# Second attention: two tiles of maxima and one unit in three PSUM banks, VectorE reduces maxima bank by bank

## The reference

```python
qkv = xn @ w_qkv
...
q = q * scale
sim = jnp.einsum('bhid,bhjd->bhij', q, k)
attn = jax.nn.softmax(sim, axis=-1)
out = jnp.einsum('bhij,bhjd->bhid', attn, v)
out = jnp.transpose(out, (0, 2, 1, 3)).reshape(b, n, DIM_INNER)
return out @ w_out
```

## Time and profile before

| what | us |
|---|---|
| median of 3 runs (lowest to highest) | 1211.06 (1207.18 to 1211.94) |
| the profiled execution, its own time | 1208.63 |
| its span from the first to the last instruction | 1206.8 |
| TensorE (PE) busy | 1151.7 (95%) |
| VectorE (DVE) busy | 843.3 (70%) |
| GpSimd (POOL) busy | 775.8 (64%) |
| ScalarE (ACT) busy | 597.7 (50%) |

### The profile page before, as it was taken

One profiled execution on the slowest core, in us unless ns is written; L12 is line 12 of the kernel. 1 busy time (PEld: TensorE's weight loads), 2 busy tenths in 40 slices (PEclk: granted clock), 3 DMA queues, 4 the chain that ended last, 5 costly groups with the idle time before them and its releaser, 6 DMA issues.

```text
span 1206.8 us, 21785 instructions
## 1 busy us (share of the span) xinstructions
PE 1151.7 (95%) x8892; PEld 731.1 (61%) x8892; DVE 843.3 (70%) x1086; ACT 597.7 (50%) x930; POOL 775.8 (64%) x495
## 2 busy tenths in 40 slices
PE   7999999998887899999999999999999999899997
PEld 6899999876664445454444544544445445457776
DVE  4765886565566577787777777778778787865553
ACT  1543334546553645555554555546555455554342
POOL 3565776753433678878878788898888888840000
PEclk9998999998998999999999999999999999999999
DMA  6000000020000020000000000000000000000000
GB/s 206 2 2 2 3 2 2 2 72 1 1 1 1 1 95 2 1 1 1 1 1 1 1 1 1 2 1 1 1 1 1 1 1 1 1 1 10 9 9 9
DMA packets 6978, 13.65 MB, mean 11 GB/s; under 512 B 1744, under 2 KB 4176, under 8 KB 6496
## 3 DMA queue, kind: packets, MB, share of 16 engines
q1 hardware_dynamic: 6096, 11.66, 2.9%
q10 hardware_dynamic: 784, 0.61, 0.2%
HBM read 11.22 MB, written 1.05 MB: 10 GB/s over the span
## 4 chain that ended last, share of the span: by engine, by line
PE 85%; DVE 8%; ACT 3%; issue 3%; ACTq 1%; POOL 0%; DVEq 0%; POOLq 0%
PE o_ps L1335 19%; PE mx_ps L1294 8%; PE ha_banks L494 7%; PE st_ps L1314 5%; PE st_ps L1317 5%; PE st_ps L1320 5%; PE bank L1693 3%; PE pj_ps L1246 3%; PE pj_ps L1265 3%; PE bank L1695 3%; PE bank L1694 3%; PE pj_ps L1257 2%; PE ha_banks L558 2%; PE ha_banks L511 2%; PE pj_ps L1240 2%
## 5 line engine op out<-in xcount | busy, mean ns | idle before, releaser
L1609 POOL TENSOR_TENSOR acc<-acc,prob 128x1024 f32<-128x1024 f32 x192 | 466.3, 2429 | 77.4 <-ACT prob L1456 68.5
L1518 DVE TENSOR_REDUCE mx_part<-mx_ps 128x2 f32<-128x1024 f32 x251 | 300.4, 1197 | 145.6 <-PE mx_ps L1294 145.6
L1456 ACT ACTIVATE prob<-st_ps 128x1024 f32<-128x1024 f32 x256 | 248.6, 1023 | 226.3 <-PE st_ps L1320 226.3
L1335 PE MATMUL o_ps<-prob,v_cur 128*64 128x512 f32 x1024 | 244.8, 599 | 0.0
L1294 PEld LDWEIGHTS mx_ps<-k_hi,q_hi 64*128 64x128 f32 x502 | 47.2, 184 | 142.3 <-issue 98.1
L1294 PE MATMUL mx_ps<-k_hi,q_hi 64*128 64x512 f32 x502 | 122.8, 485 | 8.8 <-DVE mx_part L1518 8.4
L1335 PEld LDWEIGHTS o_ps<-prob,v_cur 128*64 128x64 f32 x1024 | 65.5, 136 | 97.6 <-issue 90.8
L1534 DVE RECIPROCAL rden<-rden 128x128 f32<-128x128 f32 x128 | 120.3, 942 | 2.6 <-ACT rden L1420 2.6
L1609 POOL TENSOR_TENSOR acc<-prob 128x1024 f32<-128x1024 f32 x32 | 76.0, 2375 | 51.9 <-PE pj_ps L1242 31.2
L1320 PE MATMUL st_ps<-q_hi,d_lo 64*128 64x512 f32 x512 | 101.3, 391 | 0.0
L752 POOL TENSOR_TENSOR ha_wide<-ha_pt,ha_own 128x512 f32<-128x512 f32 x64 | 73.8, 1185 | 8.6 <-ACT ha_pt L709 8.6
(11 more groups left out here) (364 smaller groups left out, 2207.3 us busy)
## 6 DMA issues: line engine op xcount, KB each, us to landing
h_w<-in_h SPq DMA_DIRECT2D x2, 1024.0 KB, 8.0
w_raw<-in_w SPq DMA_DIRECT2D x8, 192.0 KB, 3.6
x<-in_x SPq DMA_DIRECT2D x4, 256.0 KB, 6.4
head_wkv<-in_wkv SPq DMA_DIRECT2D x1, 1024.0 KB, 10.6
out<-fin SPq DMA_DIRECT2D x4, 256.0 KB, 2.3
m_w<-in_m SPq DMA_DIRECT2D x3, 256.0 KB, 2.8
sel_raw<-in_sel SPq DMA_DIRECT2D x1, 576.0 KB, 11.3
ha_head_pos<-in_pos ACTq DMA_DIRECT2D x2, 256.0 KB, 7.8
```

Source lines behind the costliest of these rows:

```text
L1335: mm = pe.matmul(o_ps[rows(h), :], v_cur[:, m % 2, j, rows(h)], prob[:, (16 * m + slot) % RING, h, :], start=(j == 0), stop=(j == KT - 1), ...
L1456: act.activation(prob[:, n % RING, :, :], st_ps[:, slot % 2, :, :], ACT.Exp, scale=SCALE).then_inc(s_exp, 1)
L1518: dve.reduce_max(mx_part[:, :, i, keys:keys + 1], maxima_banks(q, n), AX_X).then_inc(s_mxr, 1)
L1609: pool.tensor_tensor(total, old, new, ALU.add).then_inc(s_acc, 1)
```

## The change

A batch with m of at least 1 and b not 0 or 4 is "three" (the rule `three`), up to the last tile of maxima: 6 batches in each of the steps 1 to 14 and 2 in step 15, 86 in all. In these:

- the first tile of maxima goes into `mx_ps` banks 0 and 1 as before;
- the second goes into `mx_ps` bank 0 and `pj_ps`. It waits for the reduction of bank 0 of the first tile alone (`first_out`) and for the former reader of `pj_ps`;
- the early unit goes into bank 1 of `mx_ps` (`aside`), and waits for the whole reduction of the first tile;
- the first tile of the batch after waits for both, the reductions and the reader of the early unit;
- VectorE reduces each of the four banks by an instruction of its own, 128x512.

All other batches are as they were. Since `pj_ps` has another order of users, `pj_uses` takes the place of `turns` in `bank_free`.

```diff
+    def three(m, b):
+        return m >= 1 and b % (BATCHES // 2) != 0 and BATCHES * m + b < BATCHES * (STEPS - 1) + 3
...
+    def batch_of(q, n):
+        return divmod(8 * q + n // 2 + 3 - BATCHES, BATCHES)
...
+    def apart(q, n):
+        return three(*batch_of(q, n))
...
+    first_out, all_out, count = {}, {}, 0
+    for q in range(STEPS):
+        for n in range(16):
+            first_out[q, n] = count + 1
+            count += 2 if apart(q, n) else 1
+            all_out[q, n] = count
...
     def tensor_unit(pe, q, u):
         p = q % PAIRS
-        to = pj_ps[:, :]
+        to = unit_bank(q, u)
...
+        elif aside(q, u):
+            pe.wait_ge(s_mxr, all_out[maximum(q - AHEAD[u], BEFORE.index(u), 0)])
         else:
             bank_free(pe, turn_of[q, u])
...
     def maxima_banks(q, n):
...
+        if n % 2 and apart(q, n):
+            return [mx_ps[:, 0, :], pj_ps[:, :]]
+        return [mx_ps[:, h, :] for h in range(2)]
...
     def tensor_maxima(pe, q, n):
...
+        elif n % 2 and apart(q, n):
+            pe.wait_ge(s_mxr, first_out[q, n - 1])
+            bank_free(pe, turn_of[q, ("max", n)])
         else:
-            pe.wait_ge(s_mxr, 16 * q + n)
+            pe.wait_ge(s_mxr, all_out[q, n] - (2 if apart(q, n) else 1))
+            was = divmod(8 * q + n // 2 + 2 - BATCHES, BATCHES)
+            if n % 2 == 0 and three(*was) and before(*was):
+                unit_out(pe, *before(*was))
...
     def vector_maxima(dve, q, n):
         i, keys = MX[n]
         dve.wait_ge(s_mx, 16 * q + n + 1)
-        dve.reduce_max(mx_part[:, :, i, keys:keys + 1], maxima_banks(q, n), AX_X).then_inc(s_mxr, 1)
+        if apart(q, n):
+            for h in range(2):
+                dve.reduce_max(mx_part[:, h, i, keys:keys + 1], maxima_banks(q, n)[h], AX_X).then_inc(s_mxr, 1)
+        else:
+            both = st_ps[:, 2 - n % 3, :, :] if q == 0 and n < 8 and n % 3 else mx_ps[:, :, :]
+            dve.reduce_max(mx_part[:, :, i, keys:keys + 1], both, AX_X).then_inc(s_mxr, 1)
```

More of the change, by code:

```diff
@@ L1154, in after, with maximum, maxima_there, unit_there @@
         return (q, AFTER[b]) if 0 <= q < STEPS else None
+    def maximum(m, b, second):
+        n = 2 * (BATCHES * (m + 1) + b - 3) + second
+        return (n // 16, n % 16) if 0 <= n < 16 * STEPS else None
+    def maxima_there(m, b):
+        if not three(m, b):
+            return None
+        q, n = maximum(m, b, 1)
+        return q, ("max", n)
+    def unit_there(m, b):
+        return None if three(m, b) else before(m, b)
     def norm_at(m, b):
         return [(LAST, ("norm", n)) for n in NORMS_AT.get((m, b), ()) if n in ("mean", "var", "spread", "rvar", "rspread")]
+    def three(m, b):
[10 more added lines that the diff above has]
+            all_out[q, n] = count
+    MXR_END = count
+    def aside(q, u):
+        if u not in BEFORE:
+            return False
+        b = BEFORE.index(u)
+        return three(q - AHEAD[u], b)
     turns = [(0, QK[3]), (0, QK[2]), (0, ("v", 0)), (0, ("v", 1)), (0, ("tr", 0))]
@@ L1163, in second_attention @@
               for u in [before(m, b), after(m, b)] + norm_at(m, b) if u]
[L1164 removed]
+    pj_uses = turns[:5]
+    pj_uses += [u for m in range(STEPS + 1) for b in range(BATCHES)
+                for u in [maxima_there(m, b), unit_there(m, b), after(m, b)] + norm_at(m, b) if u]
+    turn_of = {turn: n for n, turn in enumerate(pj_uses)}
     count_of = {turn: n + 1 for n, turn in enumerate([t for t in turns if t[1][0] != "norm"])}
[L1168 to L1171 removed]
     def half_of(half):
@@ L1245, in tensor_unit @@
                 for h in range(2):
-                    mm = pe.matmul(pj_ps[rows(h), tile(i)], xr[:, chunk(q, u[1]), i * P + h * HD:i * P + h * HD + HD],
+                    mm = pe.matmul(to[rows(h), tile(i)], xr[:, chunk(q, u[1]), i * P + h * HD:i * P + h * HD + HD],
                                    w_raw[:, p, W_QK:W_V], start=True, stop=True, skip_group_check=True)
@@ L1250, in tensor_unit @@
             for h in range(2):
-                mm = pe.matmul(pj_ps[rows(h), 0:P], mx_row[:, h, :], c.ident[:, :], start=True, stop=True,
+                mm = pe.matmul(to[rows(h), 0:P], mx_row[:, h, :], c.ident[:, :], start=True, stop=True,
                                skip_group_check=True)
@@ L1269, in maxima_banks @@
     def maxima_banks(q, n):
-        return st_ps[:, 2 - n % 3, :, :] if q == 0 and n < 8 and n % 3 else mx_ps[:, :, :]
+        if q == 0 and n < 8 and n % 3:
+            return [st_ps[:, 2 - n % 3, h, :] for h in range(2)]
+        if n % 2 and apart(q, n):
+            return [mx_ps[:, 0, :], pj_ps[:, :]]
+        return [mx_ps[:, h, :] for h in range(2)]
     def tensor_maxima(pe, q, n):
@@ L1385, in scalar_split, with unit_bank @@
         act.activation(w_hi[:, p, :], w_raw[:, p, 0:W_QK], ACT.Copy).then_inc(s_whi, 1)
-    def qk_bank(q, u):
-        return st_ps[:, 0, QK.index(u), :] if q == 0 and u in QK[:2] else pj_ps[:, :]
+    def unit_bank(q, u):
+        if q == 0 and u in QK[:2]:
+            return st_ps[:, 0, QK.index(u), :]
+        return mx_ps[:, 1, :] if aside(q, u) else pj_ps[:, :]
     def scalar_unit(act, q, u):
```

29 lines of the change are left out of this document (15 added, 14 removed).

## The result

The changed kernel takes **1190.23 us** (median of 4 runs, 1190.03 to 1191.22), the kernel before in the same comparison 1209.95 (1207.18 to 1211.94): a ratio of 0.984, 95% interval 0.9813 to 0.9868. The forecast was 1187, with a range of 1182 to 1198. Its profiled execution has a span of 1188.6 us against 1206.8.

A forecast was written before the change was run, and what follows sets the result against it. TensorE was taken to set the time, with losses between starts. Gains of 17.6 + 4.5 + 0.5 = 22.6 us gave 1186.0 from the profiled 1208.63, or 1188.5 from the median; 1187 was taken, range 1182 to 1198.

The forecast's parts named there:

- What bounds the kernel: Second attention: TensorE, busy for all 550 us, sets the time; the loss must come from times between starts.
- The second tile: Second tile of maxima in full batches: waiting for one bank's reduction wins 0.21 each, 84 times, 17.6 us.
- The early unit's cover of 0.16: Early unit in bank 1 of `mx_ps`: ready at 611.41, wanted at 611.57, so covered by 0.16, cost 0.
- `out`, 0.16 in 28 batches: Batches 3 and 7: `out` no longer waits for `q_max`, gaining 4.5 us, at most 1.4 us at risk.
- The next first tile: First tile of the batch after: waiting for the early unit's reader just fits, cost 0, bound 1.4 us.
- sign of being wrong: Early unit, `out` or batch 3's first tile beginning with idle time that a reduction or `q_lo` ended.
- VectorE's extra work: 172 instructions, each pair 0.06 to 0.12 longer, 10 to 20 us busy; no cost except through the releases.
- GpSimd: GpSimd's share rises from 84% to 87% as the step shrinks to about 41.4: cost 0, bound 1 us.
- Step 15: Two second tiles released 0.5 to 0.6 earlier each, but `den` then waits: 0.5 counted, bounds 0 and 1.1.
- A (1194): Rival on VectorE's split reductions: a half costs more than 0.60, such as 0.68; time 1194; chance 14%.
- B (1204): Rival on the second tile: it does not start earlier, only `out` gains 4.5 us; time 1204; chance 6%.

The follow-up runs named there:

- only_tile: The changed kernel with the rule `three` in batches 1, 2, 5 and 6 alone: 1201.32 us, ratio 0.9918 to the kernel before.
- short_first: The kernel before, with the first tile's reduction in the 86 batches taking only 256 columns of each bank: 1181.15 us, ratio 0.9764 to the kernel before.
- only_out: The changed kernel with the rule `three` in batches 3 and 7 alone: 1200.08 us, ratio 0.990 to the kernel before.
- again: The changed kernel, unchanged, measured again on another chip: 1182.18 us, ratio 0.9773 to the kernel before.

## Why the prediction was right, point by point

- **What bounds the kernel.** Right. TensorE is busy for all of the window in both, and the gain sits in times between starts that the busy time doesn't show.
- **The second tile, 0.21 in each of 84 batches.** Right: 1.39 and 0.32 for the 1.38 and 0.32 foretold, 4 x 0.215 in only_tile, and short_first shows that it is the end of the reduction that counts.
- **The early unit's cover of 0.16.** Held. The unit follows the second tile by 0.32 with the wait in place, as in the earlier trace rows; the halves that it waits for end at 609.45, 0.21 ahead of it.
- **`out`, 0.16 in 28 batches.** Right: 1.72 and 0.95, and 2 x 0.37 in only_out. The load is 0.14 ahead of its matmul where 0.10 was foretold, since halves behind each other start 0.55 apart here.
- **The next first tile.** Right in the steady steps: `q_lo` of batch 2 is done 0.18 ahead of it. **Missed in step 1**: my statement "cost 0, bound 0.1 x 14" came from steady batches alone. In step 1 VectorE has `xr_lo` between the halves and `q_lo` comes 2.6 us late for this wait. Measured 1.06, once. It is also the one place in steps 1 to 14 where TensorE showed a sign of being wrong that the prediction named: the first tile of batch 3 begins with 2.58 of idle time that `q_lo` ended.
- **VectorE's extra work.** The pair costs 0.06 more, the low end of what was taken, and nothing where it is covered.
- **GpSimd.** TensorE never waited for it in the second attention; ScalarE did once in the steady part, for 0.46 us at 892, and no step shows it. The step fell to 41.35, where 41.4 was foretold. Where GpSimd did cost time is a place that the prediction didn't look at: its addition holds up `xr_lo` in step 1.
- **Step 15.** Less than foretold: some 0.2 for 0.5. Its second tiles wait 1.55 and 1.40 (2.03 and 1.93 in the earlier trace rows), which is the 0.5 each of the prediction. But `den` then comes 2.16 after the outputs (1.77 before) and `out` 2.07 (1.72 before), and each is followed 0.05 later, so that most of the 1.0 goes back. That `den` might wait was foreseen, that `out` would come late behind `q_max` was not:

```profile
1020.64 1.08 PE L1307 MATMUL pj_ps<-acc,ones 128*64 128x512 f32 x4 [0.23 <-DVE mx_part L1585]
...
1031.15 0.65 PE L1315 MATMUL pj_ps<-o_n,wo 128*64 128x512 f32 x2 [0.18 <-DVE q_max L1565]
```

- **The rivals' times.** A (1194) and B (1204) are reckoned from 1208.63, the forecast from 1209.6; on its base they would be 1195 and 1205. Neither came, so nothing hangs on it.

The sum of the mechanisms is 1.63 x 14 + 0.2 less 1.06, 22.0 us, close to the 22.6 foretold, and part of that closeness is luck: the steps gave 0.7 more than their 22.1, step 15 gave 0.3 less, and the stall that was priced at nothing took 1.06. The first comparison shows 19.7 between the medians, the span of the two profiled executions 18.2. The 3.8 us between 22.0 and 18.2 fall ahead of step 2, where the trace of the changed kernel has lower granted clocks than that of the kernel before (0.92 against 1.00 from 385 to 450 us). In `again`, with 1.00 there, the span is 1180.3, 26.5 below the trace of the kernel before. So the size that one pair of executions shows differs by 8 us while the steady step stays the same to 0.01. Why an execution is granted the one or the other, and whether the longer stall makes the low stretch behind it likelier, stays open.

## What to carry to other kernels

When the bounding engine shows 100% busy, compare the time between starts of the same sequence in two places that differ in one wait: 0.1 us of lateness and as much again for an unhidden weight load showed in no busy time, and were worth 17 us. Splitting an operation costs on its own (0.06 us a pair here) and paid here only because the first part releases something that is waited for. A wait that is moved to a place with room must be looked up in the odd iterations too, at the start and the end, where other work stands in front of it. And where total times of one kernel spread by 8 us, a steady step read from the timeline tells changes of 0.1 us apart.

## What the hardware did unexpectedly

A VectorE operation with both inputs in SBUF that starts while a GpSimd addition runs ends only after that addition is over. `xr_lo` took 2.79 us before and 2.71 after, begun 0.13 and 0.20 into additions of 2.4, and ended 0.55 and 0.56 after their ends (441.30 for 440.75, 443.31 for 442.75). Its halves of 256 columns took 2.39 and 1.24 and ended 0.28 after the additions that they had started in. The same holds for `o_n`: from 420 to 1020 us 28 such operations of each of the two traces started during an addition, and all ended 0.55 to 0.56 after it. Beside an addition of 0.22 the whole `xr_lo` took 0.63. The Trainium skill, page "SBUF — State Buffer", section "SBUF: two separate sides", says that such an operation and one of GpSimd that reads SBUF share a pair of ports, and that the one that starts first holds it for its whole length; these runs agree. Cutting the operation did not shorten it here, where it began early in an addition; what helped was an addition that is short.
